# An LSTM kernel with a state-space scan and two mixtures of experts beside it: seven moves in the order of its instructions

## The chip, the core and the metric

One core of a Trainium2 chip runs the whole program. TensorE is called PE here, VectorE DVE, ScalarE ACT, GpSimd POOL and the queue that issues the DMAs SP. The metric is the device time of one execution in microseconds (us), as the median of several executions.

## The reference, cut to what matters

Four blocks follow each other on x of shape (4, 1024, 128), each as `x = layernorm(x + block(x))`; all of it is fp32.

```python
# block 1: state space          block 3: LSTM (20 units), batch 4, 1024 steps one after the other
xz = x @ W_in.T                 g = xg[t] + h @ W_hh.T
x_d = silu(conv4(x_d))          c = sig(f) * c + sig(i) * tanh(gg);  h = sig(o) * tanh(c)
h = exp(d*A) * h + d * b * u    mu[t] = w0*mu[t-1] + w1/s + w2*(t+1)/s     # relu'd projections of h
y = (h . c + D*x_d) * silu(z)   w = exp(-(rel - mu)**2 / (2*sigma**2)), masked, normalised
                                context = w @ x
# block 2: 16 experts of 64, top 2, and a shared one of 352, gated silu
# block 4: four layers l of:    comb = top-2 softmax over 4 experts of x @ rw[l]
                                y_e = gelu(layernorm(x)*g+b @ w1[l,e] + b1) @ w2[l,e] + b2
                                x = sum_e comb_e * (x + y_e)
```

## The kernel before, in words

**Tiling.** Time is cut into 8 chunks of 128 steps; a tile holds 128 features and 4 x 128 columns, so an operation on it is 128x512. The LSTM runs through the chunks one step after the other. `period(i)` is the work of LSTM chunk i, and beside its 128 steps stand the attention and the four expert layers of chunk i-1 (`layer1_*`, layers numbered l = 0 to 3), the first mixture of chunk i+1 (`layer0_*`), the state-space scan of chunk i+2 (`mamba_scan_*`) and the preparation of the next one (`mamba_pre_*`, `mamba_soft_*`). Period 0 has no layer1, period 6 has no scan, period 7 neither scan nor layer0, and after the last LSTM step period 8 does layer1 of the last chunk alone. Ahead of period 0 `opening` does the first two scans without the LSTM.

**Order.** It is written out by hand. Each of these parts is one Python generator per engine, and every `yield` ends its share of a **slot**. `period` goes through the slots; in each it emits one LSTM step and then one share of layer1, layer0, the scan or whatever else is due. Every engine works through its instructions in that order, so a slot is as long as the slowest engine makes it, and the LSTM step of the next slot waits behind everything that was emitted before it. One LSTM step is: PE L907 (W_hh times h), ACT L917 and L918 (tanh of the gates), DVE L931, L934, L937 (the cell), ACT L921 (its tanh), DVE L942 (h, called `hist`). What PE is given in slot k it does while DVE and ACT are still at slot k-1, since its step comes first in the chain.

**Slots of a layer.** `LAYER` is 23 slots, numbered 0 to 22 here (variable `o`); the first layer begins at slot `att` = 17 + i of its period. Slots 0 to 4 are the layernorm and the choice of experts: PE takes the mean (L625, L627, or L337), DVE centres (L372), ACT squares (L362, tile `esig`), PE sums it (L347), DVE and POOL make the reciprocal root, PE spreads it over rows (L354), DVE scales (L381, tile `xhat`). In slot 4 PE also transposes the choice (L646), ACT copies it (L708) and loads the table of Gelu (L709). From slot 5 on PE makes one `w1` product a slot (L658), ACT its Gelu (L716), and PE from slot 7 one `w2` product (L668); in slot 20, with the last Gelu, ACT loads the table of Exp back (L719) in the layers 0 to 2 of periods 1 to 5. Slots 6 to 21 are **heavy**: there the scan goes on (DVE L1210 and L1219 in turn, POOL L1137, L1141, L1156, ACT L1198) and layer0 rests. ACT makes the scan's decays (L1242, `burst`) eight at a time: one in slot 22, two each in 0, 1 and 2, one in 3, each time after ACT's other work of the slot. layer0 takes the slots 22 and 0 to 5 of each layer and those ahead of and behind the four layers; of its eleven blocks (`U0`) each takes three slots: gate product and ACT's tanh (L465, L517), up product (L469), down product (L477, the last one L481). `fill_pe` (L1450) adds a matmul whose result nobody reads in slots 1 to 3, 512 columns wide or 256 (`L0_WIDE` tells where).

**Tail.** Behind the four layers comes `mamba_leave_*` (gate, output product), then `mamba_pre_*` (convolution taps L957, ...), then `mamba_soft_*`, which begins with two table loads.

## Time and profile before

| | us |
|---|---|
| three runs | 3055.70, 3059.55, 3059.56 (median 3059.55) |
| the profiled execution, its own time | 3062.91 |
| its span in the trace | 3061.1 |
| first LSTM step's `hist` at | 280.4 |
| last LSTM step's `hist` at | 2854.9 |
| busy: PE, DVE, ACT, POOL | 2498.1, 1894.9, 1388.8, 1010.2 |

The span is from the first to the last instruction; 1.8 us of the execution lie around it. Busy shares are means over stages that differ. The page has the span in 40 slices of 76.5 us, with a digit for each engine's busy tenths, and PEclk, the granted share of PE's clock in tenths (10 is 2.4 GHz, 5 is 1.2 GHz; a 9 is written for 90% and more). Between 280.4 and 2854.9 us stand the 1024 LSTM steps, 2.51 us each on average.

### The profile page before, as it was taken

How to read it: one execution, taken by the hardware profiler on the slowest of the kernel's cores; microseconds unless marked ns; L12 is line 12 of the kernel's file. 1: busy time of each engine (PE TensorE's matmuls, PEld its weight loads, DVE VectorE, ACT ScalarE, POOL GpSimd, SP SyncE). 2: the span in 40 equal slices, each digit the busy share in tenths (PEclk: the TensorE clock that was granted, in tenths of full speed). 3: DMA queues.
4: the chain of work that ended last, by engine and by line, in shares of the span. 5: the costliest groups of instructions: out<-in, count | busy, mean ns of one | idle time of the engine just before them, and what ended most of it. 6: DMA issues, size and time to landing. Idle time of an engine off the chain costs nothing.

```text
span 3061.1 us, 31112 instructions
## 1 busy us (share of the span) xinstructions
PE 2498.1 (82%) x7376; PEld 1267.5 (41%) x7376; DVE 1894.9 (62%) x6569; ACT 1388.8 (45%) x4624; POOL 1010.2 (33%) x913
## 2 busy tenths in 40 slices
PE   5677864388887998689978989699978996899598
PEld 1233442254434444444435444444444444444444
DVE  5575785467766777577756776577765555444422
ACT  3323333345544554455545554455534444344233
POOL 4343463135432554244513543244520002000200
PEclk8797556579986999699977999699968996799599
DMA  3232331012320332023211321123201210111021
GB/s 121 84 87 73 111 100 39 0 61 97 94 63 28 96 100 63 29 85 100 90 39 51 100 80 59 30 80 97 90 14 58 69 59 14 42 60 59 11 83 59
DMA packets 111776, 204.74 MB, mean 67 GB/s; under 512 B 14799, under 2 KB 24422, under 8 KB 111592
## 3 DMA queue, kind: packets, MB, share of 16 engines
q1 hardware_dynamic: 111592, 202.75, 22.0%
q8 instruction: 59, 0.97, 0.1%
q14 instruction: 125, 1.02, 0.1%
HBM read 195.36 MB, written 7.34 MB: 66 GB/s over the span
## 4 chain that ended last, share of the span: by engine, by line
PE 40%; DVE 29%; ACT 16%; issue 8%; POOL 1%; DVEq 0%; POOLq 0%; ACTq 0%
PE p_hid L658 8%; PE p_turn L907 6%; DVE state L1210 6%; ACT cell_t L921 4%; PE p_misc L668 4%; DVE cell L937 3%; DVE add_c L934 3%; PE p_acc L668 3%; DVE weighed L1219 3%; DVE p_turn L931 2%; ACT decay L1242 2%; DVE hist L942 2%; ACT cand L918 2%; PE p_gate L465 2%; PE p_hid L957 1%
## 5 line engine op out<-in xcount | busy, mean ns | idle before, releaser
L907 PEld LDWEIGHTS p_turn<-hist,w_hh 22*128 22x128 f32 x2048 | 365.4, 221 | 1087.8 <-DVE hist L942 972.9
L907 PE MATMUL p_turn<-hist,w_hh 22*128 22x4 f32 x2048 | 451.1, 288 | 402.5 <-DVE hist L942 383.2
L658 PE MATMUL p_hid<-xhat,w 128*128 128x512 f32 x1024 | 574.1, 644 | 0.1
L921 ACT ACTIVATE cell_t<-cell 20x4 f32<-20x4 f32 x1024 | 207.7, 203 | 701.4 <-DVE cell L937 701.4
L1137 POOL TENSOR_TENSOR drive<-du,rows 128x512 f32<-128x512 f32 x256 | 456.1, 1782 | 66.4 <-DVE p_turn L1210 28.5
L931 DVE SCALAR_TENSOR_TENSOR p_turn<-p_turn,cell 20x4 f32<-20x4 f32 x1024 | 170.6, 167 | 478.5 <-ACT p_turn L917 455.3
L716 ACT ACTIVATE hid<-p_hid,b1f 128x512 f32<-128x512 f32 x512 | 351.9, 687 | 234.8 <-PE p_misc L668 146.0
L388 POOL TENSOR_TENSOR n_rstd<-n_var,minus_half 128x4 f32<-128x4 f32 x56 | 62.1, 1110 | 1090.5 <-DVE n_var L376 1090.5
L1156 POOL TENSOR_TENSOR y<-y,weighed 128x512 f32<-128x512 f32 x192 | 242.7, 1264 | 424.0 <-DVE weighed L1219 423.5
L942 DVE SCALAR_TENSOR_TENSOR hist<-p_turn,cell_t 20x4 f32<-20x4 f32 x1024 | 162.6, 159 | 275.7 <-ACT cell_t L921 275.7
L917 ACT ACTIVATE p_turn<-p_turn 96x4 f32<-96x4 f32 x1024 | 157.9, 154 | 355.3 <-PE p_turn L907 352.5
L1210 DVE TENSOR_TENSOR_SCAN state<-decay,drive 128x512 f32<-128x512 f32 x192 | 275.5, 1435 | 7.0 <-ACT decay L1242 1.1
L668 PE MATMUL p_acc<-hid,w 128*128 128x512 f32 x512 | 272.8, 616 | 0.0
L668 PE MATMUL p_misc<-hid,w 128*128 128x512 f32 x512 | 261.4, 592 | 0.0
L918 ACT ACTIVATE cand<-p_turn 32x4 f32<-32x4 f32 x1024 | 171.8, 168 | 24.9
L937 DVE SCALAR_TENSOR_TENSOR cell<-p_turn,add_c 20x4 f32<-20x4 f32 x1024 | 157.9, 154 | 35.3
L658 PEld LDWEIGHTS p_hid<-xhat,w 128*128 128x128 f32 x1024 | 159.2, 190 | 41.8 <-issue 26.9
L934 DVE SCALAR_TENSOR_TENSOR add_c<-p_turn,cand 20x4 f32<-20x4 f32 x1024 | 155.0, 151 | 31.6
L1219 DVE TENSOR_TENSOR weighed<-state,rows 128x512 f32<-128x512 f32 x208 | 147.5, 709 | 2.8 <-PE p_hid L1171 0.5
L668 PEld LDWEIGHTS p_misc<-hid,w 128*128 128x128 f32 x512 | 97.3, 190 | 122.5 <-issue 75.6
L668 PEld LDWEIGHTS p_acc<-hid,w 128*128 128x128 f32 x512 | 93.1, 191 | 98.0 <-issue 58.1
L1171 PE MATMUL p_hid<-weighed,ident 128*128 128x512 f32 x128 | 83.8, 748 | 59.1 <-DVE weighed L1219 58.8
(220 smaller groups left out, 3389.0 us busy)
## 6 DMA issues: line engine op xcount, KB each, us to landing
rows<-rows_dram SPq DMA_DIRECT2D x128, 512.0 KB, 5.1
w<-w_dram SPq DMA_DIRECT2D x128, 256.0 KB, 2.6
w<-in_w2T SPq DMA_DIRECT2D x128, 256.0 KB, 2.6
comb_b<-comb_dram SPq DMA_DIRECT2D x64, 512.0 KB, 4.6
rows<-comb_dram SPq DMA_DIRECT2D x128, 128.0 KB, 2.9
w<-in_w1T SPq DMA_DIRECT2D x16, 256.0 KB, 2.7
w_dram<-w SPq DMA_DIRECT2D x16, 256.0 KB, 2.2
out_xT<-result SPq DMA_DIRECT2D x8, 256.0 KB, 2.5
```

The lines of the kernel that those rows point to most:

```text
L658: nc.tensor.matmul(p_hid[:, v % 2, :], w1[:, v // FB, (v % FB) * P:(v % FB + 1) * P], xhat[:, :], start=True, stop=True).then_inc(g_h, 1)
L668: nc.tensor.matmul((p_misc1, p_acc1)[e % 2][:, :], w2[:, e, f, :], hid1[:, w % 2, :], start=(f == 0), stop=(f == FB - 1)).then_inc(g_y, 1)
L716: nc.scalar.activation(hid1[:, v % 2, :], p_hid[:, v % 2, :], ACT.Gelu, bias=b1f[:, l * UN + v:l * UN + v + 1]).then_inc(g_gelu, 1)
L907: nc.tensor.matmul(gate_bank(i)[:, :, t:t + 1], w_hh[:, :], before, start=False, stop=False, skip_group_check=True).then_inc(gates_done, 1)
L918: nc.scalar.activation(cand[:, :], gate_bank(i)[96:128, :, t:t + 1].rearrange("p b o -> p (b o)"), ACT.Tanh)\
L921: nc.scalar.activation(cell_t[64:64 + PE_, :], cell[32:32 + PE_, :], ACT.Tanh, scale=0.5).then_inc(cell_tanh, 1)
L934: nc.vector.scalar_tensor_tensor(out=add_c[32:32 + PE_, :], in0=gate(0), scalar=1.0, in1=cand[0:PE_, :], op0=ALU.add, op1=ALU.mult).then_i ...
L937: nc.vector.scalar_tensor_tensor(out=cell[32:32 + PE_, :], in0=gate(32), scalar=0.5, in1=add_c[32:32 + PE_, :], op0=ALU.mult, op1=ALU.add) ...
L1137: nc.gpsimd.tensor_tensor(flat(drive[:, n % 2, :, :]), du[:, j, :], rows[:, (u * S + s_) % ROWS, 0, :], ALU.mult).then_inc(driven, 1)
L1156: nc.gpsimd.tensor_tensor(y[:, j, :], y[:, j, :], weighed[:, n % 2, :], ALU.add).then_inc(y_summed, 1)
L1210: nc.vector.tensor_tensor_scan(state_tile(u, k), flat(decay_tile(u, k)), flat(drive[:, n % 2, :, :]), 0.0, ALU.mult, ALU.add).then_inc(sca ...
L1219: nc.vector.tensor_tensor(weighed[:, n % 2, :], state_tile(u, k), rows[:, (u * S + s_) % ROWS, 1, :], ALU.mult).then_inc(weighed_done, 1)
```

## The change

1. **Decays first**: `burst` is advanced ahead of layer1 and layer0, not behind them.
2. **First mixture off a layer's last slot**: layer0 rests in slot 22 too, and starts one slot earlier (`L0_AT` 4 to 3); it thus has six slots a layer instead of seven. `L0_WIDE` is set anew.
3. **Last projection set back**: layer0's last down product comes two slots later, and what follows it one more (`FOLD` and POOL's count go with it).
4. **Tables**: the load of Exp moves from slot 20 to slot 21.
5. **Transposes**: the choice is transposed in slot 5, behind the first `w1` product and into `p_acc1`; ACT's copy goes from slot 4 to slot 6, and SP's store and reload of it one slot later.
6. **Means and statistics**: the four projections for mu come in the order 0, 2, 1, 3; 1/T goes into the weights, so that one DVE operation falls away in each chunk; the four scans of mu stand in two slots, and bn_stats and bn_aggr in two.
7. **Convolution spread**: taps, z products and ACT's parts of `mamba_pre` are put in 13 steps instead of 11, and `mamba_leave` in one more.

```diff
@@ layer0_pe
+        yield
+        yield
         pe.wait_ge(hidw_done, (q + 1) * U0)
         nc.tensor.matmul(acc0_bank(q)[:, :], w_down[:, U0 - 1, :], hid0w[:, (U0 - 1) % 2, :],
                          start=False, stop=True).then_inc(down_done, 1)
+        yield
         yield
@@ layer0_dve
         weigh(U0 - 1)
+        for _ in range(3):
+            yield
         dve.wait_ge(down_done, (q + 1) * U0)
@@ layer1_pe
-                if s_ == 4:
-                    pe.wait_ge(g_comb, n + 1)
-                    for j in range(B):
-                        mm = nc.tensor.transpose(p_hid[0:E1, 1, j * P:(j + 1) * P], comb1[:, j, :], ident[:, :])
-                    mm.then_inc(g_combT, 1)
@@
+                if v == 0:
+                    pe.wait_ge(g_comb, n + 1)
+                    for j in range(B):
+                        mm = nc.tensor.transpose(tile(p_acc1, j)[0:E1, :], comb1[:, j, :], ident[:, :])
+                    mm.then_inc(g_combT, 1)
@@ layer1_act
                 if s_ == 4:
-                    act.wait_ge(g_combT, n + 1)
...
-                    nc.scalar.copy(combT1[:, :], p_hid[0:E1, 1, :]).then_inc(g_combT_taken, 1)
                     act.preload_act_table(ACT.Gelu)
@@
-                    if v == UN - 1 and l < L - 1 and q + 3 < NCH:
-                        act.preload_act_table(ACT.Exp)
+                if v == 1:
+                    act.wait_ge(g_combT, n + 1)
...
+                    nc.scalar.copy(combT1[:, :], p_acc1[0:E1, :]).then_inc(g_combT_taken, 1)
+                if v == UN and l < L - 1 and q + 3 < NCH:
+                    act.preload_act_table(ACT.Exp)
@@ layer1_dve
-        nc.vector.tensor_scalar(mw[:, 1, :], p_hid[:, 1, :], 0.0, 1.0 / T, ALU.max, ALU.mult).then_inc(mup_taken, 1)
...
+        nc.vector.scalar_tensor_tensor(out=mdrive[:, :], in0=p_hid[:, 0, :], scalar=0.0, in1=mdrive[:, :],
+                                       op0=ALU.max, op1=ALU.add).then_inc(mup_taken, 1)
...
-        nc.vector.tensor_tensor(mdrive[:, :], mdrive[:, :], mw[:, 1, :], ALU.add).then_inc(m_step, 1)
...
+        mu_scan((0, 1))
+        yield
+        mu_scan((2, 3)).then_inc(mu_done, 1)
@@ mamba_pre_pe
+        yield
+        yield
         taps(0, (0, 1))
         yield
-        yield
-        taps(0, (2, 3))
+        taps(0, (2,))
+        yield
+        taps(0, (3,))
@@ period
+            o = (slot - att) % LAYER
+            if u < NCH and layer1 and att - 1 <= slot < tail - 2:
+                for _ in range({22: 1, 0: 2, 1: 2, 2: 2, 3: 1}.get(o, 0)):
+                    next(burst, None)
             if layer1:
                 next(layer1, None)
...
-            if layer0 and not (heavy and slot < CH) and slot >= (L0_AT if layer1 else 0):
+            last = layer1 is not None and att < slot < tail and o == LAYER - 1
+            if layer0 and not ((heavy or last) and slot < CH) and slot >= (L0_AT if layer1 else 0):
...
-                if layer1 and att - 1 <= slot < tail - 2:
-                    for _ in range({22: 1, 0: 2, 1: 2, 2: 2, 3: 1}.get(o, 0)):
-                        next(burst, None)
```

**On the engines.** The rows are from period 3; `p_turn`, `cand` and `cell_t` are the LSTM step. ACT, second layer, slots 20 and 21, before and then in the change (`hid` is the Gelu, `carry` the scan's copy):

```order
L917 ACTIVATE p_turn<-p_turn 96x4
L918 ACTIVATE cand<-p_turn 32x4
L921 ACTIVATE cell_t<-cell 20x4
L716 ACTIVATE hid<-p_hid,b1f 128x512
L719 ACT_TABLE_LOAD
L1198 COPY carry<-state 128x4
L917 ACTIVATE p_turn<-p_turn 96x4
```

```order
L928 ACTIVATE p_turn<-p_turn 96x4
L929 ACTIVATE cand<-p_turn 32x4
L932 ACTIVATE cell_t<-cell 20x4
L718 ACTIVATE hid<-p_hid,b1f 128x512
L1215 COPY carry<-state 128x4
L928 ACTIVATE p_turn<-p_turn 96x4
L929 ACTIVATE cand<-p_turn 32x4
L932 ACTIVATE cell_t<-cell 20x4
L726 ACT_TABLE_LOAD
```

The load stood behind a Gelu; now it stands alone in the next slot. ACT in slot 1 of the third layer, before and then in the change (`esig` is the square of the layernorm, `decay` two of the scan's decays):

```order
L921 ACTIVATE cell_t<-cell 20x4
L362 ACTIVATE esig<-mdrive 128x512
L1242 ACTIVATE decay<-delta,a_neg 128x4x127 x2
L917 ACTIVATE p_turn<-p_turn 96x4
L918 ACTIVATE cand<-p_turn 32x4
```

```order
L932 ACTIVATE cell_t<-cell 20x4
L1259 ACTIVATE decay<-delta,a_neg 128x4x127 x2
L362 ACTIVATE esig<-mdrive 128x512
L928 ACTIVATE p_turn<-p_turn 96x4
L929 ACTIVATE cand<-p_turn 32x4
```

The square now waits behind both decays. PE at the end of the four layers, slots 112 and 113 of the period, before and then slots 112 to 114 in the change (`w_tap` is the convolution, `du,w_out` the scan's output product):

```order
L907 MATMUL p_turn<-hist,w_hh 128x4
L625 MATMUL p_misc<-part,mean_w 128x512
L627 MATMUL p_misc<-terms,mean_w 128x512
L481 MATMUL p_turn<-hid0w,w_down 128x512
L957 MATMUL p_hid<-xin,w_tap 128x512 x2
L907 MATMUL p_turn<-hist,w_hh 128x4
```

```order
L918 MATMUL p_turn<-hist,w_hh 128x4
L631 MATMUL p_misc<-part,mean_w 128x512
L633 MATMUL p_misc<-terms,mean_w 128x512
L465 MATMUL p_gate<-mid_x,w_gate 128x512
L918 MATMUL p_turn<-hist,w_hh 128x4
L469 MATMUL p_up<-mid_x,w_up 128x512
L918 MATMUL p_turn<-hist,w_hh 128x4
L347 MATMUL p_acc<-mean_w,esig 128x1 x4
L477 MATMUL p_turn<-hid0w,w_down 128x512
L1291 MATMUL p_hid<-du,w_out 128x512 x2
L968 MATMUL p_hid<-xin,w_tap 128x512 x2
```

The first mixture ends later in the period, and its last product and the taps no longer share a slot with the two products of the mean.

## Rows read from the trace of the kernel before

**Rows 1.** The page: span, busy times, granted clock in 40 slices, chain by engine.
```profile
span 3061.1 us, 31112 instructions
...
PE 2498.1 (82%) x7376; PEld 1267.5 (41%) x7376; DVE 1894.9 (62%) x6569; ACT 1388.8 (45%) x4624; POOL 1010.2 (33%) x913
...
PEclk8797556579986999699977999699968996799599
...
PE 40%; DVE 29%; ACT 16%; issue 8%; POOL 1%; DVEq 0%; POOLq 0%; ACTq 0%
```

**Rows 2.** Timeline, period 5, a bare LSTM step: start us, us, engine line op tiles [idle before].
```profile
2252.04 0.16 DVE L942 SCALAR_TENSOR_TENSOR hist<-p_turn,cell_t 20x4 f32<-20x4 f32 x1 [0.27 <-ACT cell_t L921]
...
2253.86 0.16 DVE L942 SCALAR_TENSOR_TENSOR hist<-p_turn,cell_t 20x4 f32<-20x4 f32 x1 [0.27 <-ACT cell_t L921]
```

**Rows 3.** Timeline, period 3, slots 19 and 20 of a layer; then line L719 alone.
```profile
1361.53 0.16 DVE L942 SCALAR_TENSOR_TENSOR hist<-p_turn,cell_t 20x4 f32<-20x4 f32 x1 [0.27 <-ACT cell_t L921]
...
1363.91 0.16 DVE L942 SCALAR_TENSOR_TENSOR hist<-p_turn,cell_t 20x4 f32<-20x4 f32 x1 [0.27 <-ACT cell_t L921]
1364.10 1.39 DVE L1210 TENSOR_TENSOR_SCAN state<-decay,drive 128x512 f32<-128x512 f32 x1
...
1364.84 1.28 ACT L719 ACT_TABLE_LOAD   x1
...
1366.24 0.15 ACT L917 ACTIVATE p_turn<-p_turn 96x4 f32<-96x4 f32 x1
...
1367.23 0.16 DVE L942 SCALAR_TENSOR_TENSOR hist<-p_turn,cell_t 20x4 f32<-20x4 f32 x1 [0.27 <-ACT cell_t L921]
...
L719 ACT ACT_TABLE_LOAD  x15: 1283/1283/1283, 696.4 to 2167.6; - x15
```

**Rows 4.** Windows, span and busy by engine, PEclk: period 4, slots 20 to 22; single layers.
```profile
core 0: us, PE busy (x) PEld busy (x) DVE busy (x) ACT busy (x) POOL busy (x), PEclk, DMA share, GB/s
...
1698.00:1701.40 3.40, 1.48 (x5) 0.59 (x4) 2.10 (x6) 2.60 (x6) 2.76 (x3) 0.99 0.01 2
1701.40:1708.00 6.60, 6.55 (x10) 3.00 (x11) 4.44 (x12) 2.27 (x8) 1.26 (x1) 0.50 0.26 95
...
1369.60:1428.10 58.50, 52.65 (x163) 24.56 (x162) 44.81 (x148) 32.55 (x109) 30.30 (x26) 1.00 0.33 99
...
1033.10:1092.30 59.20, 53.94 (x162) 25.30 (x162) 44.88 (x148) 32.56 (x109) 30.31 (x26) 0.96 0.33 103
...
2112.50:2172.30 59.80, 54.07 (x165) 24.82 (x163) 44.90 (x147) 32.55 (x108) 30.31 (x26) 0.98 0.28 89
```

**Rows 5.** Timeline, period 3, slots 1 and 2 of a layer: ACT, then PE.
```profile
1433.98 0.63 ACT L362 ACTIVATE esig<-mdrive 128x512 f32<-128x512 f32 x1
1434.51 1.31 ACT L1242 ACTIVATE decay<-delta,a_neg 128x508 f32<-128x508 f32 x2
...
1433.54 0.59 PE L1450 MATMUL p_hid<-w_gate,mean_w 128*128 128x256 f32 x2
...
1434.66 1.05 PE L347 MATMUL p_acc<-mean_w,esig 128*128 128x1 f32 x8
```

**Rows 6.** Timeline, ACT in slot 4: period 3, then period 7.
```profile
1441.99 0.57 ACT L708 COPY combT<-p_hid 4x512 f32<-4x512 f32 x1
...
2739.82 0.57 ACT L708 COPY combT<-p_hid 4x512 f32<-4x512 f32 x1 [1.28 <-PE p_hid L646]
...
2741.70 0.15 ACT L917 ACTIVATE p_turn<-p_turn 96x4 f32<-96x4 f32 x1
```

**Rows 7.** Timeline, period 3, tail: PE at the last projection; then who ended its waits.
```profile
1548.06 1.10 PE L481 MATMUL p_turn<-hid0w,w_down 128*128 128x512 f32 x2 [1.57 <-DVE hid0w L548]
...
  DVE hid0w L548: 27.3, 14
```

**Rows 8.** Timeline, period 8, PE ahead of w1; then the DVE operation that goes.
```profile
2906.71 1.06 PE L646 MATMUL p_hid<-ident,comb 128*4 128x128 f32 x4
...
L730 DVE TENSOR_SCALAR mw<-p_hid x8: 691/692/693, 600.3 to 2858.9; 128x512 f32<-128x512 f32 x8
```

More of the change, by code:

```diff
@@ L519, in layer0_act @@
                 yield
-        yield
+        for _ in range(4):
+            yield
         yield from norm_act(n0, 2 * q + 1)
@@ L588, in layer1_pe @@
         pe.wait_ge(xm_done, min(q + 3, NCH))
-        for g in range(4):
-            if g >= 2:
-                pe.wait_ge(mup_taken, q * 4 + (g - 1))
-            nc.tensor.matmul(p_hid[:, g % 2, :], w_mub[:, g, :], hist[:, q % 2, :, :], start=True, stop=True).then_inc(mup_done, 1)
+        for k, g in enumerate((0, 2, 1, 3)):
+            if k >= 2:
+                pe.wait_ge(mup_taken, q * 4 + (k - 1))
+            nc.tensor.matmul(p_hid[:, k % 2, :], w_mub[:, g, :], hist[:, q % 2, :, :], start=True, stop=True).then_inc(mup_done, 1)
             yield
@@ L894, in layer0_pool @@
         yield from norm_pool(n0, 2 * q)
-        for _ in range(6 + 3 * U0):
+        for _ in range(9 + 3 * U0):
             yield
@@ L1003, in mamba_pre_act @@
         act = nc.scalar
-        yield
-        yield
+        for _ in range(5):
+            yield
         act.wait_ge(conv_done, u * NB + 1)
@@ L1035, in mamba_pre_sp @@
     def mamba_pre_sp(u):
-        for _ in range(8):
+        for _ in range(10):
             yield
@@ L1247, in mamba_leave_act @@
         save_carry(u, NS - 1)
-        for _ in range(3):
+        for _ in range(4):
             yield
@@ L1451, in fill_pe @@
                          start=True, stop=True)
-    L0_WIDE = {1, 5, 7, 49, 51} | set(range(11, 46))
+    L0_WIDE = {1, 5, 7, 46, 48, 52, 54} | set(range(11, 44))
     def period(i, of, soft):
```

69 lines of the change are left out of this document (36 added, 33 removed).

## The prediction

> **What bounds the kernel now.** I read the page first. Over the whole span no engine is full: PE is busy 82% and DVE 62%, and the chain that ended last runs 40% over PE, 29% over DVE, 16% over ACT [rows 1]. That is a ring, not one engine: the LSTM step. The digits of the granted clock show that PE is not at one level either; they lie between 5 (all at 1.2 GHz) and 9 [rows 1]. Next I looked at one bare step in the timeline. From one `hist` to the next it takes 1.82 us when nothing else is due [rows 2]. 1024 of these would be 1864 us; the steps take 2574.5 us (280.4 to 2854.9), so some 710 us are added by what stands between the steps. The question in each slot is therefore which engine reaches its next step instruction late.
>
> The rule for that comes from slots in which one engine decides. Slot 19 has a 0.75 and a 0.68 us operation on DVE and takes 2.38 us; slot 20 has a scan of 1.39 us on DVE, which alone would give the same 2.4, but takes 3.32 us, because ACT has a Gelu, then a table load of 1.28 us and a small copy ahead of the gates' tanh, which starts at 1366.24 [rows 3]. So a slot costs about 1.0 us plus DVE's other work, or about 1.0 us plus ACT's, or PE's own sum with some 0.3 us for the step, whichever is most, and never under 1.8. One us saved on an engine that does not decide is worth nothing.
>
> The third view is the clock. In period 4 the slot with the table load holds 1.48 us of PE work in 3.40 us, and then the granted clock is 0.50 for the next stretch, in which the means of the next layer stand [rows 4]. A layer of period 3 in which the clock stays at 1.00 takes 58.5 us; seven layers of periods 2, 4 and 5 have such a fall at their beginning, the first of them 59.2 us long, the last 59.8 [rows 4]. I put a fall at 1 to 2.5 us.
>
> **The change, part by part.** All is summed against the profiled execution (3062.9 us, of which 3061.1 are its span), which is 3.4 us over the median of the three runs; I take those off at the end.
>
> *Table of Exp, slot 20 to 21.* Fifteen loads [rows 3]. In slot 20 ACT's 1.28 us go and DVE's scan decides: 3.32 to 2.42, minus 0.90. In slot 21 DVE has two operations of 0.69 and already needs 2.4 us; ACT has nothing there but the load, 1.0 + 1.28 = 2.3, hidden. 15 x 0.90 = **-13.5**. Ends: 0, were slot 21 to grow as much, and 15 x 1.28 = -19. In the trace the gates' tanh follows 0.12 us after the load's end at 1366.12, with a small copy between [rows 3], so 1.28 is the whole price. The Trainium skill ("ScalarE: Activation LUTs", What ACT_TABLE_LOAD costs) puts a switch at 2.66 us, as it adds a drain of 1.38 us to a load of 1.283; by that slot 21 would need 3.7 us, and the term would be near +5. This case's rows have the load and not the drain.
>
> *The clock behind that slot.* What preceded the fall in period 4 was a PE idle for most of a 3.3 us slot [rows 4]. At 2.4 us the same product fills more of it. But slot 22 loses layer0's product as well, so two slots in a row now hold one product each. I take half of the falls as gone: 7 x 1.05 = 7.4, **-7**. Ends: 0 and 7 x 2.5 = -17.
>
> *layer0 off slot 22, and ACT's order in slot 0.* DVE's 2.1 us of other work in slot 22 become 1.45: -0.69 there, in 24 boundaries of layers. PE, however, has two means, the logits and a layer0 product in slot 0, 3.8 us in a row, and that chain does not get shorter. I keep 0.45 of each boundary in periods 1 to 5 (where ACT's tanh of layer0 no longer has two decays of 0.65 [rows 5] behind it, and the copy goes from slot 4) and 0.7 in period 6: 20 x 0.45 + 4 x 0.7 = **-12**. Ends: 0 and 24 x 1.2 = -29.
>
> *Copy and transposes.* In slot 4 ACT loses a copy of 0.57 us [rows 6]. In period 7 it even waits 1.28 us for the transposes [rows 6]: table load and xhat can now start at once, 1.8 us earlier, but then the copy stands in slot 6 and four transposes lie between two w1 products; I keep 1.0 x 4 = **-4**. Where layer0 is present PE becomes the one that decides slot 5 (w1 product, transposes of 0.44, layer0's product), which gives back what slot 4 gained; that is in the 0.45. In slot 6 the copy of 0.57 comes beside a Gelu and a scan of DVE: 0.1 x 20 = **+2**. In period 8 nothing hid behind ACT: the transposes run while DVE makes xhat, 1.06 us at the low clock [rows 8]; behind the change they stand between products that decide, 4 x 0.5 = **+2**. SP stores and reloads the choice one slot later, and the first reader is in slot 11, five slots on; I cost it at nothing. If the DMAs came late, DVE's weighting in slot 11 would wait.
>
> *Last projection.* PE waits 1.57 us for DVE's last weighting, with the taps queued behind it and the LSTM's product behind those; all such waits add up to 27.3 us in 14 entries, in which load and product of one projection both count, so 13 us at most [rows 7]. With two slots between them the wait goes. Half of it was on the ring: **-6**; ends 0 and -13. What becomes late next is layer0's norm: it now ends three to six slots further on, in slots that were bare (1.82 us) and at 1.2 GHz; five ends of periods at 0.6, **+3**.
>
> *Means, statistics, convolution, decays' neighbours in the attention stage.* One DVE operation of 0.69 us goes from each of eight chunks [rows 8], at most -5.5. But the scan's preparation slides two slots into the attention stage of the next period and meets layer0's norm there. I take **-2**, with ends -6 and +5.
>
> *Decays ahead of the square.* This is the part that I fear. Before, `esig` came first, at 1433.98, and PE's sums of it began at 1434.66, 0.2 us after the step's product; the two decays of 1.31 us came behind it [rows 5]. Now the square is 1.3 us later. PE waits that long in slot 2, behind it are layer0's product, the filler and the LSTM's next product. In slot 2 ACT has two more decays and a tanh, so the ring had about 1.3 us of slack on PE: the wait itself costs next to nothing. But PE is idle, next to eight products of a single column, and I expect the clock to fall at some of the 20 boundaries; 10 x 1.5 = **+15**. Ends: 0, and 20 x 2.3 = +46.
>
> Sum: -13.5 - 7 - 12 - 4 + 2 + 2 - 6 + 3 - 2 + 15 = -22.5. 3062.9 - 22.5 = 3040.4, less 3.4: **3037 us**.
>
> **Rivals.** *The clock holds* (the price of the square's delay is nought, and the falls behind slot 20 all go): -22.5 - 15 - 8 = -45.5, **3014 us**. For it: the filler in slots 1 to 3 is there, half as wide but just ahead of the wait [rows 5]. Against it: the two thin slots 21 and 22.
>
> *The clock falls at nearly every boundary* (the slower side). One mechanism, in slots 1 and 2: PE idle from the filler's end to the late square. It decides from about 15 of 20 boundaries at 2.3 us: at all 20, -22.5 - 15 + 7 + 46 = +15.5, **3075 us**. For it: in period 4 a similar stretch was enough [rows 4]. The Trainium skill ("TensorE: Matmul & The Clock Gate", Part 1) says that throttled is the default state and activity releases it, which points the same way. Against it: a later fall may lie beside ACT's decays, and costs little there.
>
> *The gains are absorbed.* Only the tables and period 7 count, since PE decides slots 0 and 5: -13.5 - 4 + 4 + 3 + 7 = -3.5, **3056 us**. For it: PE is 82% busy [rows 1]. Against it: the rule of the slots fits DVE and ACT well.
>
> *A table load costs its drain too*: the first term turns from -13.5 to +5, about **3055 us**; the rows speak against it.
>
> **How the numbers follow.** Forecast 0.50, the clock holds 0.20, absorbed 0.15, falls everywhere 0.12, drain 0.03. 0.2% (6.1 us) is about what a measurement of this kernel can tell from no change. Below 3053.4 lie the forecast, the held clock and a little of the absorbed case: faster 0.74. Same 0.14, slower 0.12. The forecast's own range is 3022 to 3050. The range that should hold 8 in 10 reaches from 3010, under the held clock, to 3062, over the absorbed case; the clock that falls everywhere stays outside.
>
> **What would show it.** Right: slot 20 at 2.4 us and slot 21 unchanged, in all 15 layers; no wait of PE for `hid0w` at the last projection; PE idle 1.3 us longer in slot 2 for `esig`. Layers of periods 1 to 5 at 56 to 58 us. Wrong: slot 21 at 3 us or more; the mean granted clock of these layers under 0.95, or at 1.00 throughout; a weighting in slot 11 that waits for a DMA; a tail or attention stage longer by more than 3 us in each period.

## The result, and the profile after

Four runs of the changed kernel took 3081.2 to 3085.4 us, median 3083.0, against 3055.7 to 3059.6 us (median 3058.8) for the kernel before on the same chip. The ratio is 1.0081 with a 95% interval of 1.0067 to 1.0095: slower by 0.8%, where 3037 us were forecast. A second set of six runs, taken later beside the experiments, gave 1.0060 (1.0036 to 1.0083). Two single executions among all the runs, of 3886 and 3898 us, were in a slow state and count in no ratio. The profiled execution took 3081.2 us, 18.3 us more than that of before.

The page of the changed kernel (span, busy times, granted clock in 40 slices, chain by engine), against [rows 1]:

```profile
span 3079.4 us, 31114 instructions
...
PE 2571.1 (83%) x7376; PEld 1297.2 (42%) x7376; DVE 1898.8 (62%) x6562; ACT 1387.6 (45%) x4624; POOL 1018.8 (33%) x913
...
PEclk8796556579995999699968999598969995789588
...
PE 43%; DVE 31%; ACT 11%; issue 7%; POOL 1%; DVEq 0%; POOLq 0%; ACTq 0%
```

The count of PE's instructions is the same as before, 7376, and PE is busy 73 us longer. The same matmuls run longer, so the granted clock was lower; ACT's share of the chain went down from 16 to 11%, PE's up from 40 to 43%. The change did take work off ACT's path, and PE gave it back.

**What went as forecast.** The table load, timeline of period 3, ACT first and then DVE, against [rows 3]:

```profile
1426.59 0.69 ACT L718 ACTIVATE hid<-p_hid,b1f 128x512 f32<-128x512 f32 x1 [0.26 <-PE p_acc L674]
...
1428.77 1.28 ACT L726 ACT_TABLE_LOAD   x1
1430.06 0.15 ACT L928 ACTIVATE p_turn<-p_turn 96x4 f32<-96x4 f32 x1
```

```profile
1426.36 0.16 DVE L953 SCALAR_TENSOR_TENSOR hist<-p_turn,cell_t 20x4 f32<-20x4 f32 x1 [0.27 <-ACT cell_t L932]
1426.55 1.39 DVE L1227 TENSOR_TENSOR_SCAN state<-decay,drive 128x512 f32<-128x512 f32 x1
...
1428.78 0.16 DVE L953 SCALAR_TENSOR_TENSOR hist<-p_turn,cell_t 20x4 f32<-20x4 f32 x1 [0.27 <-ACT cell_t L932]
...
1431.10 0.16 DVE L953 SCALAR_TENSOR_TENSOR hist<-p_turn,cell_t 20x4 f32<-20x4 f32 x1 [0.27 <-ACT cell_t L932]
```

From `hist` to `hist`, slot 20 takes 2.42 us (3.32 before) and slot 21, with the load, 2.32. The gates' tanh starts 0.01 us behind the load's end. PE's waits for `hid0w` at the last projection are gone from the table of waits.

**What came in its place.** The square in slot 1 of a layer, the same timeline, ACT and then PE, against [rows 5]:

```profile
1436.88 1.33 ACT L1259 ACTIVATE decay<-delta,a_neg 128x508 f32<-128x508 f32 x2
1438.12 0.61 ACT L362 ACTIVATE esig<-mdrive 128x512 f32<-128x512 f32 x1
```

```profile
1436.56 0.59 PE L1469 MATMUL p_hid<-w_gate,mean_w 128*128 128x256 f32 x2
1437.11 0.38 PE L918 MATMUL p_turn<-hist,w_hh 22*128 22x4 f32 x2
1438.78 1.26 PE L347 MATMUL p_acc<-mean_w,esig 128*128 128x1 f32 x8 [1.30 <-ACT esig L362]
1439.90 2.05 PE L477 MATMUL p_turn<-hid0w,w_down 128*128 128x512 f32 x2
1441.75 1.06 PE L1469 MATMUL p_hid<-w_gate,mean_w 128*128 128x256 f32 x2
1442.74 0.44 PE L918 MATMUL p_turn<-hist,w_hh 22*128 22x4 f32 x2
```

PE idles 1.30 us, does eight products of one column, and then layer0's product (two instructions of 512 columns) takes 2.05 us and the filler 1.06, where two such instructions took 1.02 and a filler 0.59 at the high clock. The LSTM's product waits behind them until 1442.74. PE's waits for the square, from the table of waits, were 4 before (3.8 us, all in period 8); now there are 21, 17 of them in the layers of periods 1 to 5:

```profile
PE p_acc L347 <- ACT esig L362: 23.6, 21, 1.6
```

The windows that follow (span, then busy time by engine, then the granted clock) are this stretch of the layer, and a whole layer of period 7:

```profile
1438.80:1443.11 4.31, 4.31 (x15) 2.61 (x15) 1.59 (x7) 1.91 (x6) 2.46 (x3) 0.60 0.02 5
...
2679.49:2734.05 54.56, 53.02 (x148) 25.29 (x148) 23.78 (x125) 24.15 (x89) 1.01 (x1) 0.87 0.18 58
```

The interval between two steps that took 2.4 us is 4.5 us long here, with PE busy throughout. Counted over the granted clock of the two traces, in the layers of periods 1 to 5 before there are 9 stretches at 1.2 GHz that begin there, 44 us in sum; after there are 20, 96 us in sum, and 15 of the 20 begin while PE is at its slots 2 and 3. Over these 20 layers PE's busy share went from 0.89 to 0.68 in its slot 22, and from 0.93 to 0.67 in slot 2.

Where the 18.3 us come from, by the steps of the prediction. "Measured" is the difference of the two traces, from the starts of the 1024 `hist` writes:

```
part of the program                            forecast   measured
opening and period 0                               0        +4.8
layers, periods 1-5: slot of the table load      -13.5      -13.5
layers, periods 1-5: slots 22 and 0 to 5          +1        +9.2
layers, periods 1-5: all other slots               0        +5.3
layers, period 6                                  -2.8      -4.0
layers, period 7                                  -4        +6.3
attention stages, periods 1-7                     -2        +8.9
tails, periods 1-7                                -3        -5.7
period 8                                          +2        +7.0
sum                                              -22.3     +18.3
```

Slots are those of ACT and DVE here; the time from one `hist` to the next then has PE's work of the slot that follows. The +9.2 are a sum of large parts: where PE is at slot 0, -12.2; at slot 3, +17.6; at slot 4, +5.0; at slots 5 and 6, -10.7 and +9.2, which nearly cancel; at slots 1 and 2, +0.2.

Four of these are seen in rows. The end, PE ahead of w1 in period 8, against [rows 8]:

```profile
2918.24 2.07 PE L657 MATMUL p_hid<-xhat,w 128*128 128x512 f32 x2 [0.78 <-DVE xhat L381]
2920.11 1.06 PE L662 MATMUL p_acc<-ident,comb 128*4 128x128 f32 x4
2920.96 3.54 PE L657 MATMUL p_hid<-xhat,w 128*128 128x512 f32 x4
2924.33 1.02 PE L674 MATMUL p_misc<-hid,w 128*128 128x512 f32 x2
```

Before:

```profile
2907.70 3.98 PE L658 MATMUL p_hid<-xhat,w 128*128 128x512 f32 x6
2911.51 1.02 PE L668 MATMUL p_misc<-hid,w 128*128 128x512 f32 x2
```

w1 starts behind a wait of 0.78 us for `xhat` that the transposes filled before, and w2 follows 6.1 us after w1's start where it took 3.8. The transposes between two w1 products take 0.85 us, and the clock stays low longer. Windows that end with w2's start, before and then after, and two parts of after:

```profile
2898.00:2911.50 13.50, 12.11 (x36) 7.99 (x37) 3.45 (x24) 4.08 (x6) 1.01 (x1) 0.57 0.05 19
```

```profile
2908.50:2924.30 15.80, 13.59 (x36) 8.58 (x37) 3.45 (x24) 4.00 (x7) 1.01 (x1) 0.50 0.00 1
...
2917.00:2924.30 7.30, 6.52 (x13) 2.71 (x12) 0.69 (x1) 1.83 (x3) 0.00 (x0) 0.50 0.00 0
2924.30:2955.00 30.70, 29.14 (x79) 13.45 (x77) 8.53 (x31) 11.75 (x17) 0.56 (x1) 1.00 0.36 104
```

In the attention stage of period 5, ACT:

```profile
1938.94 0.60 ACT L684 ACTIVATE esig<-p_hid 128x512 f32<-128x512 f32 x1 [0.96 <-PE p_hid L598]
1939.55 1.28 ACT L1087 ACT_TABLE_LOAD   x1
1940.85 1.15 ACT L1087 ACTIVATE y<-y 128x512 f32<-128x512 f32 x2
1942.01 1.28 ACT L1088 ACT_TABLE_LOAD   x1
1943.31 0.15 ACT L928 ACTIVATE p_turn<-p_turn 96x4 f32<-96x4 f32 x1
```

The softplus of the scan's preparation slid by two slots and now stands behind `esig`, which waits 0.96 us for PE as it did before: this slot takes 6.3 us. The opening, where layer0's norm of chunk 0 now runs two slots later beside the scan (PE's waits for the weighted state were 1.45 and 0.89 us at this place):

```profile
228.47 2.07 PE L1188 MATMUL p_hid<-weighed,ident 128*128 128x512 f32 x2 [2.81 <-DVE weighed L1236]
...
235.20 2.07 PE L1188 MATMUL p_hid<-weighed,ident 128*128 128x512 f32 x2 [3.16 <-DVE weighed L1236]
```

And one of four of the "other slots" that were 2.4 us and are now 3.65; DVE, then POOL:

```profile
1086.54 2.28 DVE L1227 TENSOR_TENSOR_SCAN state<-decay,drive 128x512 f32<-128x512 f32 x1 [0.37 <-issue]
```

```profile
1086.47 1.26 POOL L1154 TENSOR_TENSOR drive<-du,rows 128x512 f32<-128x512 f32 x1
```

The scan takes 2.28 us in place of 1.39 when POOL's product of the next drive starts just ahead of it (1086.47 against 1086.54). Four of these at 1.2 us make 4.9 of the 5.3.

### The profile page after: what moved, and what is told of

It is laid out like the page before. It is cut to its first block, busy times and chain, and to the rows that moved or that the text cites. A ratio compares the mean times of both kernels' runs of the same rounds, so it can differ in the third digit from the quotient of the medians.

```text
span 3079.4 us, 31114 instructions
## 1 busy us (share of the span) xinstructions
PE 2571.1 (83%) x7376; PEld 1297.2 (42%) x7376; DVE 1898.8 (62%) x6562; ACT 1387.6 (45%) x4624; POOL 1018.8 (33%) x913
## 3 DMA queue, kind: packets, MB, share of 16 engines
q14 instruction: 125, 1.02, 0.1%
## 4 chain that ended last, share of the span: by engine, by line
PE 43%; DVE 31%; ACT 11%; issue 7%; POOL 1%; DVEq 0%; POOLq 0%; ACTq 0%
PE p_hid L657 9%; DVE state L1227 7%; PE p_turn L918 6%; ACT cell_t L932 4%; PE p_misc L674 4%; DVE cell L948 3%; DVE add_c L945 3%; DVE weighed L1236 3%; DVE p_turn L942 2%; PE p_acc L674 2%; PE p_up L469 2%; PE p_gate L465 2%; PE p_turn L477 2%; DVE terms L834 2%; DVE hist L953 2%
## 5 line engine op out<-in xcount | busy, mean ns | idle before, releaser
L657 PE MATMUL p_hid<-xhat,w 128*128 128x512 f32 x1024 | 583.4, 653 | 6.6 <-DVE xhat L381 5.7
L1154 POOL TENSOR_TENSOR drive<-du,rows 128x512 f32<-128x512 f32 x256 | 448.2, 1751 | 63.9 <-DVE p_turn L1227 29.5
```

The costliest lines, as they stand in the source:

```text
L657: nc.tensor.matmul(p_hid[:, v % 2, :], w1[:, v // FB, (v % FB) * P:(v % FB + 1) * P], xhat[:, :], start=True, stop=True).then_inc(g_h, 1)
L1154: nc.gpsimd.tensor_tensor(flat(drive[:, n % 2, :, :]), du[:, j, :], rows[:, (u * S + s_) % ROWS, 0, :], ALU.mult).then_inc(driven, 1)
```

## The experiments

Each run stands beside runs of the kernel before on the same chip, and the ratio is to those, with its 95% interval. An interval n here is the time from the `hist` of step n-1 of a layer to that of step n: PE's work of slot n lies in it, and ACT's and DVE's of slot n-1. The expectations that follow count slots in this way where they speak of falls and thin slots.

### Is it the late square?

`square_first`, the changed kernel with two decays of one slot behind layer 1's work:

```diff
-                for _ in range({22: 1, 0: 2, 1: 2, 2: 2, 3: 1}.get(o, 0)):
+                for _ in range({22: 1, 0: 2, 1: 2, 3: 1}.get(o, 0)):
...
+                if layer1 and att - 1 <= slot < tail - 2:
+                    for _ in range({2: 2}.get(o, 0)):
+                        next(burst, None)
```

> Theory A (the clock): what costs in the layers is that the square comes behind two decays, PE idles 1.1 to 1.3 us ahead of its sums (21 such waits, 23.6 us) and the granted clock falls there; the slot that follows takes 4.0 to 4.5 us where it took 2.4. With the square back ahead of the two decays of its own slot alone (the other decays stay first) the waits go from 21 to 4, the falls at slots 2 to 4 of the layers of periods 1 to 5 go too, and each layer of periods 1 to 5 loses 1 to 2 us: 3050 to 3062 us against 3083. Theory B (order on ACT costs nothing, the loss is outside the layers, at the opening, in periods 7 and 8 and in the attention stages): the waits go but the time stays within 5 us of 3083. Theory C (clock falls are merely moved: some other thin slot of the boundary gets them): waits 4, as many falls as now, 3075 to 3083.

`decays_behind`, the whole move undone, all other moves kept (the three lines of the burst go back to where they were):

> All decays back behind layer 1's work on ACT, the other moves kept. Theory A: like the kernel with only the square first, within 5 us of it: 3050 to 3065. If decays first was worth something in slots 22, 0, 1 and 3, this one is up to 8 us slower than the square-first kernel. Theory B: 3078 to 3088.

`decays_alone`, the kernel before with this move alone:

> The kernel before with this one move alone: all decays ahead of layer 1's work on ACT. Theory A: waits for the square of 1 us or more at some 17 to 20 boundaries, falls there, 20 boundaries at 1 to 2 us more: 3078 to 3098 us, slower by 0.6 to 1.3%. Theory B: 3052 to 3064, no change.

Measured: `square_first` 1.0058 (1.0038 to 1.0077), 20 waits for the square. The edit missed: the decays ahead of the square are those of slot 1, and it moved those of slot 2. It tells only that the place of these two makes no difference that can be seen beside 1.0060 and 1.0081. `decays_behind` 1.0032 (1.0013 to 1.0050), 3072.0 us, 4 waits, and 12 falls with 51 us at the low clock where the changed kernel has 20 and 96 (its profiled execution, 3061.0 us, is 11 us shorter than its median). The step-to-step time with PE's slot 3 is back at 2.69 us on the mean of the 20 layers (3.56 in the changed kernel, 2.68 before). So the order of the decays costs some 0.3 to 0.5%, and the kernel is still slower than before; 3050 to 3065 was expected. `decays_alone` 1.0004 (0.9989 to 1.0019): no change to be seen, though the waits are there in full, from its table of waits:

```profile
PE p_acc L347 <- ACT esig L362: 27.4, 24, 1.6
```

It has 9 falls in the layers, as many as the kernel before. The 20 waits of 1.2 us in the layers cost nothing there that can be seen. Theory A, that the late square by itself brings the clock down, has fallen; so has "the wait costs".

### The wait or the clock?

`filler_ahead`, the changed kernel, square late as it is:

```diff
                 fill(CT >> wide)
+                if o == 1:
+                    fill(CT)
```

> The changed kernel with one more filler product of 512 columns (0.85 us at the high clock, 24 more in periods 1 to 7 per slot-1 place) behind slot 1, just ahead of the wait for the square. The square stays late. Theory A (it is the idle PE and its clock that cost): PE's waits for the square shrink from 1.1 to 1.3 us to about 0.3, falls at slots 2 to 4 go in at least half of the layers, 3060 to 3073 us. Rival D (it is the delay of PE's queue behind the wait that costs): the queue behind starts no earlier, 3080 to 3095.

Measured: 0.9955 (0.9938 to 0.9971), 3048.6 us, below every expectation. The waits are as many, and shorter:

```profile
PE p_acc L347 <- ACT esig L362: 8.9, 21, 1.6
```

PE has 28 products of 512 columns more, which nobody reads, and the kernel is 1.0 to 1.2% faster than the changed one. The time at the low clock in the layers of periods 1 to 5 went from 96 to 44 us, the layers themselves from 1174.7 to 1157.8. What stands behind the wait starts no earlier: PE's sums of the square begin 2.02 us after the `hist` of the LSTM's step in slot 1, against 1.94 without the filler, on the mean of the 20 layers. What differs is the clock. The kernel before was not run with fillers, so how much they would win there is not known.

### The other half: the last slot

`last_slot_back` gives layer0 its product in slot 22 again; `filler_last` puts a filler there in its place:

```diff
-            if layer0 and not ((heavy or last) and slot < CH) and slot >= (L0_AT if layer1 else 0):
+            if layer0 and not (heavy and slot < CH) and slot >= (L0_AT if layer1 else 0):
```

```diff
+            if fill and last and slot < CH and i < NCH:
+                fill(CT)
```

> The changed kernel with layer0's product back in a layer's last slot (slot 22), everything else as changed, the late square too. Theory E (the falls come from the two ingredients together: thin slots 21 and 22 without layer0's product, and then the square that comes 1.1 to 1.3 us late): the falls in the layers of periods 1 to 5 go from 20 to 12 or fewer, as in the kernel with decays first alone (9), and the layers of these five periods from 1175 us to about 1160 to 1168; 3065 to 3076 us on this chip, where the changed kernel would take about 3083 to 3087. Theory A (the late square alone): 18 or more falls, 3080 to 3092.

> The changed kernel with one filler product of 512 columns in a layer's last slot, in the place of layer0's product, the square late as it is. PE is busy 1.4 of 2.3 us in that slot, so the filler's 0.85 us fit. Theory E: 12 falls or fewer, 3055 to 3072 us (layer0's product does not come back, so slots 22 and 0 stay as short as they are). Theory A: the falls at slots 2 and 3 stay, 3080 to 3090.

The edit of `last_slot_back` also shifts which fillers are wide, as they are counted by layer0's steps. Measured: 1.0000 (0.9980 to 1.0020), 3059.2 us, faster than either expectation; 15 falls, more than expected, but 68 us low, and the layers at 1161.0 us as expected. `filler_last` 0.9954 (0.9934 to 0.9973), 3045.4 us, again better than expected; 17 falls, but short ones, 58 us low. Theory E holds in the time, not in the count: it is how long the clock stays low that is paid for. Taking back the thin last slot wins back the whole loss, taking back the late square about half. But the two do not need each other, as Theory E has it. Mean times of an interval in the 20 layers, by intervals 1 and 3:

```
run               interval 1   interval 3
before                  4.01         2.68
decays_alone            3.43         2.95
changed kernel          3.95         3.56
decays_behind           4.36         2.69
last_slot_back          2.92         3.74
filler_last             3.67         3.24
```

Each ingredient has its own place: with the product back in slot 22 interval 1 is short and interval 3, behind the late square, as long as in the changed kernel; with the decays back it is the other way round. Why interval 3 is slow in `last_slot_back` and hardly so in `decays_alone`, which has the same product in slot 22 and the same late square, was not tried.

These runs hold the cleanest evidence on the clock. In period 7 there is no layer0 and no burst, so `last_slot_back` has the same instructions in the same order there as the changed kernel. One layer of it, and the same in `filler_last` (windows, columns as in [rows 4]):

```profile
2663.00:2712.13 49.13, 47.06 (x148) 22.22 (x148) 23.75 (x125) 24.19 (x89) 1.01 (x1) 1.00 0.20 65
```

```profile
2663.45:2713.07 49.62, 47.84 (x151) 22.59 (x150) 23.79 (x124) 24.19 (x89) 1.01 (x1) 1.00 0.20 65
```

49.1 us at a granted clock of 1.00, against 54.56 at 0.87 above, with the same 148 matmuls and ACT's same 24 us. Even inside this one execution both are seen: the last three layers of its period 7 take 49.1, 49.2 and 54.6 us. Period 7 as a whole takes 297.9 us in the changed kernel, 131 of them at the low clock, and 286.5 here, 106 of them low, with the same instructions. Without the filler it can go either way; with it, period 7 took 283.1 us, and 279.9 and 286.2 in the two kernels with both fillers.

### The moves that were costed at little

`transposes_back`, `conv_back` and `last_projection_back` each take one move back and keep the rest.

On PE in `transposes_back` (ACT's copy and SP's store and reload go back with it):

```diff
                 next(ln)
+                if s_ == 4:
+                    pe.wait_ge(g_comb, n + 1)
...
+                    mm.then_inc(g_combT, 1)
```

In `conv_back`, with the pauses of its four routines:

```diff
-    PRE = 13
+    PRE = 11
...
-    SCAN, LEAVE = 2 * NS, 4
+    SCAN, LEAVE = 2 * NS, 3
```

In `last_projection_back`, with ACT's and DVE's pauses:

```diff
-        yield
-        yield
         pe.wait_ge(hidw_done, (q + 1) * U0)
...
-        for _ in range(9 + 3 * U0):
+        for _ in range(6 + 3 * U0):
```

> The changed kernel with the four transposes and their copy back ahead of w1. If they are what costs at the end: from the last step to the end 206 to 208 us where the changed kernel takes 213, and period 7 at 293 to 296 where it takes 298; in sum 8 to 11 us, 3072 to 3077 us. If the end is longer for another reason (the means, the clock by chance): 211 to 214 us and 3080 to 3086.

> The changed kernel with the convolution, the preparation and the leaving of the scan at their old length (three slots fewer). If their slide is what costs: the opening at 281 to 283 us where the changed kernel takes 286.6, and the attention stage of period 5 at 62 to 64 us where it takes 68.3, in sum 6 to 10 us, 3074 to 3079 us. If nothing of it comes from there: 3080 to 3087 and both stretches as they are.

> The changed kernel with the last projection, its norm and the pauses around them where they were. The opening of the changed kernel is 2 to 8 us longer in every variant so far that has this move (282.4 to 288.4 us, 280.4 before) and layer0's norm meets the opening scan there two slots later. If the move is the cause: opening at 280 to 282 us; PE's waits for the last weighting come back, tails 3 to 6 us longer; sum near nought, 3080 to 3090 us. If not: opening at 285 to 288 and 3086 to 3095.

Measured: `transposes_back` 1.0059 (1.0036 to 1.0081), 3075.3 us; from the last step to the end 207.0 us (213.3), period 7 294.0 (297.9), as expected. So the move costs 6 us in period 8, where 2 were forecast; the 11 traces with this move have 211.7 to 213.7 us there, the seven without it 206.0 to 207.6. `conv_back` 1.0098 (1.0075 to 1.0121), 3087.9 us: the expectation was wrong. The opening stays at 287.3 us, the attention stages get 7.5 us shorter, 3.8 of them in period 5, and the tails 14.6 us longer. The spread convolution is worth more in the tails than its slide costs. `last_projection_back` 1.0034 (1.0018 to 1.0049), 3069.0 us: the opening is 277.6 us (286.6), and the tails are 11.5 us longer. The traces of all kernels with this move have an opening of 282.4 to 288.4 us, those without it 277.6 to 281.8, so this move is what lengthened it. A near balance, 3080 to 3090 us, was expected and did not come: by the ratio the kernel is 0.3 to 0.5% faster with the move taken back, as much as with the decays taken back. Where it wins this is not shown; the runs spread from 3058.7 to 3084.9 us, and the profiled one is the slowest.

### The table load alone

```diff
-                    if v == UN - 1 and l < L - 1 and q + 3 < NCH:
-                        act.preload_act_table(ACT.Exp)
+                if v == UN and l < L - 1 and q + 3 < NCH:
+                    act.preload_act_table(ACT.Exp)
```

> The kernel before with the Exp table load one slot later and nothing else. By the prediction's term the slot of the load goes from 3.3 to 2.4 us and the next stays, 15 x 0.9 = 13.5 us, and some of the seven falls behind it go: ratio 0.993 to 0.997 to the kernel before. If the falls only lie elsewhere or grow: 0.997 to 1.001. If the load is not hidden in its new slot: above 1.001.

Measured: 0.9954 (0.9938 to 0.9970), 3047.5 us, 12 us faster: inside the expected span, and one seventh of the change does better than the whole. Its interval 21 is 2.42 us on the mean, 4 falls are left of 9, and interval 1 went from 4.01 to 3.47 us. Two layers of its period 3, one with a fall and one without:

```profile
1362.97:1421.48 58.51, 54.24 (x163) 25.33 (x162) 44.82 (x147) 32.46 (x109) 30.29 (x26) 0.97 0.34 99
1421.48:1478.44 56.96, 52.32 (x162) 24.56 (x162) 44.88 (x148) 32.90 (x110) 31.25 (x26) 1.00 0.31 98
```

### Towards a version that beats both

`filler_last_transposes` joins two edits shown above:

> The changed kernel with the filler in a layer's last slot and the transposes and copy back ahead of w1. By the two runs apart (0.9954 and a gain of 0.2% from the transposes): end at 206 to 207 us, ratio 0.991 to 0.994 to the kernel before, 3030 to 3040 us. If the copy in slot 4 of ACT brings the falls back: 0.995 to 1.000.

`filler_both` joins the two fillers:

> The changed kernel with both fillers, the one of a layer's last slot and the one ahead of the late square. If the clock is what is left in the layers: fewer than 8 falls in those of periods 1 to 5, 1150 to 1156 us for them (1160 and 1158 with one filler each), ratio 0.992 to 0.995. If PE's added work costs as much as the clock gives: 0.995 to 0.999.

Measured: `filler_last_transposes` 0.9989 (0.9975 to 1.0003), 3057.5 us, not the sum of its parts. The end is at 206.0 us as expected, but period 7 is back at 298.2 (283.1 with the filler alone) and interval 5 of the layers at 3.19 us (2.50). Why the clock does not hold in period 7 with this order was not tried. `filler_both` 0.9895 (0.9874 to 0.9916), 3031.5 us: 6 falls and 20 us low, layers 1150.5 us. A layer of its period 3 and one of its period 7:

```profile
1364.33:1420.83 56.50, 53.23 (x164) 24.99 (x164) 44.24 (x147) 32.40 (x109) 30.75 (x26) 0.99 0.36 103
2651.28:2701.23 49.95, 48.56 (x153) 23.03 (x152) 23.82 (x124) 24.11 (x89) 1.01 (x1) 1.00 0.21 64
```

The last four runs ask how steady the loss is, whether layer0's start matters, and whether the other moves are needed at all:

On `filler_both`, for `filler_both_start`:

```diff
-    L0_AT = 3
+    L0_AT = 4
```

On `table_alone`, for `table_filler` (`table_decays_fillers` has the decays first and the edit of `filler_ahead` as well):

```diff
+            if fill and layer1 and not layer0 and att < slot < tail and o == LAYER - 1 and slot < CH and i < NCH:
+                fill(CT)
```

> The changed kernel itself, beside this chip's runs of the kernel before, in as many rounds as the others. If its loss is a property of the program: ratio 1.006 to 1.010 and 18 or more falls in the layers of periods 1 to 5. If it hangs on how the clock happens to lie: anything from 0.998 to 1.010, and another number of falls.

> The best so far, the changed kernel with both fillers (0.9895), and layer0 begun in slot 4 of a period again where the change begins it in slot 3. If this start is what makes slot 9 of the attention stage 4.4 us long where it took 2.7: that slot back at 2.7, attention stages at 380 to 384 us in sum (389), ratio 0.986 to 0.989. If the work only lands one slot later: attention stages within 2 us of 389, tails up to 5 us longer, 0.989 to 0.993.

> The kernel before with the table load one slot later and, in period 7 alone, a filler product in a layer's last slot, where PE has no product of layer0. The table alone gave 0.9954. If the filler holds the clock in period 7 as it does in the changed kernel (layers there 202 to 205 us in place of 214): 0.991 to 0.994. If not: 0.995 to 0.998.

> The same, with the decays ahead of the square as well and one filler product of 512 columns ahead of the late square. If the order of the decays is worth something once PE's wait is filled: waits for the square at 0.3 us each, 4 falls or fewer, layers of periods 1 to 5 at 1140 to 1147 us, ratio 0.987 to 0.992, as good as the changed kernel with both fillers though three quarters of the change are left out. If the product of 0.85 us is too much beside layer0's: 0.993 to 1.000.

Measured: `changed_again` 1.0060 (1.0036 to 1.0083), 22 falls, six runs from 3065.9 to 3090.9 us: the loss is the program's own, its size varies from run to run. `filler_both_start` 0.9892 (0.9873 to 0.9911), 3027.4 us: slot 9 of the attention stage takes 1.9 to 3.2 us again in periods 1 to 6 (3.8 to 5.0 with both fillers alone), and slot 10 has 4.1 to 4.3 instead in periods 3, 4 and 6; the stages take 389.9 us in sum, 389.3 with both fillers alone. The rival of that expectation was right in that the work only lands later, but the tails are 7 us shorter, not longer. `table_filler` 0.9963 (0.9949 to 0.9977): the filler did not hold the clock in period 7 here (layers 215.6 us), a miss. `table_decays_fillers` 0.9927 (0.9910 to 0.9944), 3035.4 us, just beside the expected span: 3 falls, and waits for the square of 13.8 us in 23, twice as long as expected.

All together, in the order of the ratio (low: us at 1.2 GHz in stretches that begin in the layers of periods 1 to 5):

```
run                      ratio    low   layers 1-5   period 7   end
filler_both_start        0.9892    20     1141.5      286.2    213.0
filler_both              0.9895    20     1150.5      279.9    212.7
table_decays_fillers     0.9927    10     1141.7      292.3    207.6
filler_last              0.9954    58     1160.0      283.1    211.7
table_alone              0.9954    20     1147.2      293.1    206.2
filler_ahead             0.9955    44     1157.8      284.2    213.7
table_filler             0.9963    34     1155.5      295.0    207.1
filler_last_transposes   0.9989    44     1165.3      298.2    206.0
before                   1         44     1173.8      293.1    206.2
last_slot_back           1.0000    68     1161.0      286.5    213.2
decays_alone             1.0004    41     1168.0      296.6    206.1
decays_behind            1.0032    51     1159.8      295.7    213.1
last_projection_back     1.0034   116     1179.7      295.4    213.0
square_first             1.0058    99     1182.0      297.9    213.2
transposes_back          1.0059   123     1193.5      294.0    207.0
changed_again            1.0060    92     1167.8      297.9    213.3
changed kernel           1.0081    96     1174.7      297.9    213.3
conv_back                1.0098   116     1171.6      295.6    213.1
```

The ratio is from all runs, the other columns from one profiled execution each, and a single execution can lie 10 us off its kernel's median, in `last_projection_back` 16.

## Why the prediction was wrong

It named the right fear and priced it in the wrong step. The five experiments that take one move back from the changed kernel give each move's price in it; the ranges are from the two ratios of the changed kernel, 1.0060 and 1.0081, and each ratio has an interval of 4 to 7 us to either side:

```
move                            forecast   price in the changed kernel
decays ahead of the square        +15        +9 to +15
layer0 off slot 22                -12       +18 to +25
last projection set back           -3        +8 to +14
copy and transposes                 0         0 to +7
convolution (part of the -2)        -2       -12 to -5
```

By its own steps:

- **Layer0 off slot 22.** This is the step that failed. "Ends: 0 and 24 x 1.2 = -29" has no price for the clock. The step before it had written that "two slots in a row now hold one product each", and had answered that only by taking half of seven old falls as gone (-7), with no new ones. The sum has -12; the move costs 18 to 25 us. Of these, 7 to 14 are in the layers of periods 1 to 5 (1161.0 us with the move taken back, 1174.7 and 1167.8 with it) and 11 in period 7, where the edit changes no instruction and only the clock differs. `filler_last` leaves the move in and fills the empty slot, and gives 0.9954. The gain was there in part: the time with PE's slot 0 fell by 12.2 us.
- **Decays ahead of the square.** The term was right in size: +15 forecast as ten falls of 1.5 us, 9 to 15 measured; 15 falls begin while PE is at slots 2 and 3, and the times with PE's slots 3 and 4 grew by 22.6 us, 1.5 for each. That "the wait itself costs next to nothing" was right too (`decays_alone`). But it was in part luck, as the same move on the kernel before costs nothing at all (1.0004), and the prediction has nothing that would tell the two cases apart. The rival with the chance of 0.12, "the clock falls at nearly every boundary", came near in number, 3075 us against 3083, with the right kind of cause. That nearness is luck for the larger part: it gave the late square all of the loss, and 27 of the 40.6 us below lie outside the layers of periods 1 to 5.
- **Table of Exp.** Right, to a tenth: -13.5 forecast, -13.5 measured, and -12 us in all when done alone. The ring's rule, 1.0 us plus the other work of the engine that decides, held for slots 20 and 21. The rows had the load and not the drain of the Trainium skill ("ScalarE: Activation LUTs", What ACT_TABLE_LOAD costs), and the result agrees with them: the slot with the load takes 2.32 us.
- **The clock behind that slot.** Right where the table moves alone (9 falls to 4). In the change as a whole the emptied slot 22 takes it back, as said above.
- **Copy and transposes.** Period 7 was forecast at -4 and period 8 at +2; the layers of period 7 came to +6.3 and period 8 to +7.0. That PE's four transposes had filled a wait for `xhat` ahead of w1 was in the prediction ("the transposes run while DVE makes xhat"). That the clock would then come back later was not. In period 7 the -4 was sound but for the clock: `last_slot_back`, with the same instructions there, has its layers at 209.3 us, 5.1 less than before.
- **Last projection.** The tails won 5.7 us, near the forecast. The opening has the same code for chunk 0, and was not costed at all: +6.2 us. Of a step that is moved, each place where it is issued counts. The rest of this move's price is not found.
- **Attention stages.** -2 forecast, +8.9 measured, 5.9 of them in period 5, where the softplus and `esig` meet in one slot. `conv_back` wins 3.8 of the 5.9 back. The ends -6 and +5 did not reach it.
- **The rest** (boundaries of period 6, SP's store and reload) went as said; no weighting waited for a DMA. So did the signs that were named for "right": slot 20 at 2.4 us, slot 21 no longer, no wait for `hid0w`, 1.3 us idle ahead of the square. They watch single moves, and all held in a kernel that got slower. The one on the whole failed: the layers of periods 1 to 5 take 58.7 us on the mean, not 56 to 58, with a mean granted clock of 0.95, at the edge named for "wrong".

Of the 40.6 us between forecast and trace, the layers of periods 1 to 5 hold 13.5, the attention stages 10.9, period 7's layers 10.3, period 8 5.0 and the opening with period 0 4.8, less 3.9 in the tails and period 6. How much the clock can give back is told by `filler_both`, which keeps all seven moves: its profiled execution is 42 us shorter than the changed kernel's, 24 of them in the layers of periods 1 to 5 and 18 in period 7. It is also 28 to 32 us faster than the kernel before, more than the 22.5 that were forecast for the change. That does not show that the change is worth this much: the kernel before has falls too (9, 44 us), and it was not run with the two fillers.

What stays open: that comparison; a kernel with both the decays and layer0's slot 22 taken back, which would tell whether their prices add up; whether the moves beside the table's, the decays' and the fillers are worth anything in sum. With them and both fillers the ratio is 0.9892 to 0.9895, without them 0.9927, and the intervals touch. Also open is why a fall's stretch is short in one kernel and long in another; PE's own idle time was the only thing varied here.

## What to carry to other kernels

Where PE is not the bound but its clock is, cost a list of small moves as one: sum up, slot by slot, how long PE stays idle in the whole stretch. A move that takes PE's work out of a slot has a price there even if it shortens the slot. A filler product in the idle slots is a cheap probe that separates "the wait costs" from "the clock costs", and it may be the fix: here it turned 0.6 to 0.8% slower into 1.05% faster. And try the best-founded move alone before the bundle; here it won 12 us by itself, while the bundle that contains it lost 20 to 24.

## What the runs showed of the hardware

- The same instructions in the same order took 49.1 us at a granted clock of 1.00 and 54.6 at 0.87, in two programs that differ only ahead of that place and also inside one execution: three layers of period 7 in a row take 54.6 us each in the changed kernel, and 49.1, 49.2 and 54.6 in `last_slot_back`.
- 56 products of 512 columns that nobody reads made the kernel faster by 1.6 to 1.8% against the changed one: 0.9895 against 1.0060 and 1.0081.
- With both fillers added to the changed kernel, 75 us less at the low clock (96 to 20) went with layers of periods 1 to 5 that are 24 us shorter: about a third of a microsecond for each.
- ACT's next instruction started 0.01 us behind the end of a table load of 1.28 us.
- DVE's scan of 128x512 took 2.28 us in place of 1.39 while POOL's product of the same size ran beside it from 0.07 us earlier. In both traces every scan behind 110 us that began 0.01 to 0.37 us after such a product (23 before, 30 after) ended 2.34 to 2.36 us after the product's start, as if it had waited for it. Five early ones in each, between 42 and 101 us, began as close behind and took 1.22 to 1.23 us; what sets them apart was not looked into.
